# Second attention: the lower half of the mask is added by GpSimd to the rectified scores instead of by TensorE to the scores

## What is computed

```python
def _L1_gnn_ref(hidden, adj, a0, a1, a2, a3):
    def edge_score(a):
        s = jnp.einsum('bid,bjd->bij', hidden * a, hidden)
        return jax.nn.leaky_relu(s, LEAKY_SLOPE)          # slope 0.2
    ...
    alpha = jnp.where(adj == 1, e0, NEG_INF)
    ...
    alpha = jax.nn.softmax(alpha, axis=-1)
    return jnp.matmul(alpha, hidden)
...
x = x + _L1_gnn_ref(_layernorm(x, axis=-1), adj, L1_gnn_a0, ...)
```

## Time and profile before

| what | value |
|---|---|
| median of three runs | 1112.4 us (1112.0 to 1114.0) |
| the profiled execution, first to last instruction (its span; the page gives no other time for it) | 1111.8 us |
| TensorE busy | 1035.5 us, 93% |
| VectorE, ScalarE, GpSimd busy | 678.5, 766.1, 383.3 us |
| `one_kind`, first mask product of batch 0 to 750 us, then 8 us of tail | 466 to 758 us |

### The profile page before, as it was taken

The page is one execution under the profiler, slowest core; times in us unless marked ns, Lnnn a source line. Parts: engine busy times, 40 slices in busy tenths (PEclk is TensorE's granted clock), DMA queues, the critical chain, the costliest instruction groups (busy, mean ns, idle before and its releaser), DMA issues. The chain is left out here.

```text
span 1111.8 us, 19991 instructions
## 1 busy us (share of the span) xinstructions
PE 1035.5 (93%) x6481; PEld 744.2 (67%) x6481; DVE 678.5 (61%) x2122; ACT 766.1 (69%) x1155; POOL 383.3 (34%) x468
## 2 busy tenths in 40 slices
PE   4788789888899999799999999999999999999998
PEld 3455556555477777478888888886466666666667
DVE  4678888778544345288999999772533333333336
ACT  4998798786565554488888888885656556565561
POOL 4113778878573413446565653201000000000000
PEclk9899999899999999899999999999999999999999
DMA  8877987723246665322333232200000000000001
GB/s 290 338 273 272 385 321 294 276 96 125 81 150 228 202 192 169 106 70 83 89 89 89 86 85 74 66 30 1 1 10 11 10 18 12 11 16 14 10 15 33
DMA packets 69145, 131.15 MB, mean 118 GB/s; under 512 B 9918, under 2 KB 30764, under 8 KB 68012
## 3 DMA queue, kind: packets, MB, share of 16 engines
q1 hardware_dynamic: 60268, 111.96, 29.5%
q0 software_dynamic: 8192, 16.79, 5.0%
q10 hardware_dynamic: 576, 1.05, 0.3%
HBM read 77.60 MB, written 52.17 MB: 117 GB/s over the span
## 5 line engine op out<-in xcount | busy, mean ns | idle before, releaser
L2346 PEld LDWEIGHTS eY<-Vo,dGW 128*128 128x128 f32 x1024 | 132.4, 191 | 54.1 <-issue 52.8
L541 POOL DMA_INDIRECT sorted_x<-V,AT_I x128 | 125.5, 980 | 57.8 <-issue 37.0
L2346 PE MATMUL eY<-Vo,dGW 128*128 128x128 f32 x1024 | 134.2, 276 | 0.1
L2329 PE MATMUL eU<-XTN,V 128*128 128x512 f32 x256 | 130.9, 593 | 0.9 <-PEq L2264 0.9
L2516 DVE TENSOR_TENSOR dGW<-H,WBC 128x512 f32<-128x512 f32 x80 | 55.3, 692 | 124.9 <-PE eY L2346 124.7
L2337 PE MATMUL eU<-H,V 128*128 128x512 f32 x256 | 131.1, 594 | 0.0
L730 PE MATMUL O<-Y,HS 128*128 128x512 f32 x256 | 127.6, 618 | 0.0
L1947 POOL DMA_INDIRECT W<-sorted_y,ROW_I x96 | 96.8, 1009 | 73.4 <-PE f_T L2021 53.4
L2425 ACT ACTIVATE H<-eU,bn 128x512 f32<-128x512 f32 x128 | 99.5, 777 | 25.5 <-PE eU L2329 16.2
L2048 PEld LDWEIGHTS f_O<-f_XN,f_PT 128*128 128x128 f32 x896 | 106.8, 192 | 12.7 <-DVE X L2159 10.3
L2048 PE MATMUL f_O<-f_XN,f_PT 128*128 128x128 f32 x896 | 109.8, 276 | 2.6 <-DVE X L2159 2.0
(11 more groups left out here) (306 smaller groups left out, 2069.9 us busy)
## 6 DMA issues: line engine op xcount, KB each, us to landing
XTN<-in_adj SPq DMA_DIRECT2D x64, 512.0 KB, 7.1
masks<-NMW SPq DMA_DIRECT2D x8, 2048.0 KB
f_MK<-masks SPq DMA_DIRECT2D x60, 256.0 KB, 2.7
sorted_y<-zero SPq DMA_DIRECT2D x39, 256.0 KB
NMW<-sorted_x SPq DMA_DIRECT2D x39, 256.0 KB, 2.6
sorted_y<-NMW SPq DMA_DIRECT2D x39, 256.0 KB, 2.5
X<-in_x SPq DMA_DIRECT2D x8, 512.0 KB, 8.0
out_x<-X SPq DMA_DIRECT2D x16, 256.0 KB, 2.3
```

The costliest lines, as they stand in the source:

```text
L541: g_.indirect_dma_start(sorted_x, bass.IndirectOffsetOnAxis(ap=AT_I[b % 2][:, kt:kt + 1], axis=0), XR[b % 2][:, t * P:(t + 1) * P], None). ...
L2329: pe.matmul(U1[j % 2][:, :], V1[:, e * P:(e + 1) * P], XTN[:, b * N + q * HALF:b * N + (q + 1) * HALF], start=True, stop=True).then_inc(u1 ...
L2346: i = pe.matmul(Y[q][:, t * P:(t + 1) * P], GW[:, j % 2, t * P:(t + 1) * P], Vo[:, e * P:(e + 1) * P], start=(e == 0 and t == 0), stop=(e ...
```

## The change

The product `bar` is gone from TensorE. GpSimd adds the lower half of the mask to the lower half of R4, in place (`bar_low`), as VectorE goes on doing with the upper half; the minimum waits for both. The rectification thus sees unmasked scores in both halves. ScalarE's copies of upper blocks now wait for the end of all scores. On GpSimd the lower add of a tile stands ahead of that tile's other work; gathers have lost their own wait for the scores, and the roots stand ahead of the gather of r=4 and r=5 in place of behind that of r=3 and r=4 (in batch 0 the one root moves to r=5).

```diff
@@ gpsimd
+                def bar_low(g):
+                    if g == 0:
+                        pool.wait_ge(late_loaded, 16 * E // 2 * (len(late_loads) + 1))
+                    if g >= RING:
+                        pool.wait_ge(loaded[g % RING], 16 * (g // RING))
+                    pool.wait_ge(r4_ready, g + 1)
+                    nc.gpsimd.tensor_tensor(R4[:, g % 2, 0:HALF], R4[:, g % 2, 0:HALF], mask(g)[:, 0:HALF], ALU.add
+                                            ).then_inc(barred_low, 1)
+
                 for b in range(B):
                     for r in range(NT):
+                        bar_low(b * NT + r)
                         if b + 2 < B:
...
-                            pool.wait_ge(t_ready, b * NT + r + 1)
+                        if r == (5 if b == 0 else 4) and b < LAST:
+                            root(b + 1)
+                        if r == 5 and b > 0:
+                            root_next(b - 1)
+                        if b + 2 < B:
                             gather(b + 2, (r,))
                         if r == 1 and b > 1:
                             feature(b - 2)
-                        if r == 3 and b < LAST:
-                            root(b + 1)
-                        if r == 4 and b > 0:
-                            root_next(b - 1)
@@ tensor, scores(g)
-                    def bar():
...
-                        return pe.matmul(T[g % 2][:, 0:HALF], identb[:, :], mask(g)[:, 0:HALF], start=False, stop=True,
-                                         skip_group_check=(g, 0) in raw_at)
...
-                    half(1)
-                    bar().then_inc(t_ready, 1)
+                    half(1).then_inc(t_ready, 1)
@@ scalar, keep_raw(g, h)
-                    act.wait_ge(raw_ready, raw_at[g, h])
+                    if h == 0:
+                        act.wait_ge(raw_ready, low_at[g])
+                    else:
+                        act.wait_ge(t_ready, g + 1)
@@ vector, shift(g)
                     dve.wait_ge(barred, g + 1)
+                    dve.wait_ge(barred_low, g + 1)
```

More of the change, by code:

```diff
@@ L1879, in one_kind @@
                  "ft_ready", "joined"))
-            barred = either("barred")
+            barred, barred_low = either("barred"), either("tail_barred")
             raw_ready, raw_kept = either("raw_ready"), either("raw_kept")
@@ L1916, in right @@
                 return max(r + 1, 4 * h), 4 * h + 4
-            raw_at = {}
+            raw_at, low_at = {}, {}
             for g_ in range(G):
@@ L1922, in one_kind @@
                         raw_at[g_, h_] = len(raw_at) + 1
+                        if h_ == 0:
+                            low_at[g_] = len(low_at) + 1
             block = ctx.enter_context(nc.Block(no_gpsimd_drain=True))
@@ L2003, in half @@
                         for c in range(4 * h, min(r, 4 * h + 4)):
-                            pe.matmul(T[g % 2][:, c * P:(c + 1) * P], raw(c, r), ident[:, :], start=first,
-                                      stop=False, is_transpose=True)
+                            i = pe.matmul(T[g % 2][:, c * P:(c + 1) * P], raw(c, r), ident[:, :], start=first,
+                                          stop=(c == min(r, 4 * h + 4) - 1 and r >= 4 * h + 4), is_transpose=True)
                             first = False
@@ L2009, in half @@
                             i = pe.matmul(T[g % 2][:, lo * P:(h + 1) * HALF], xta(b)[:, r * P:(r + 1) * P],
-                                          xt(b)[:, lo * P:(h + 1) * HALF], start=first, stop=(h == 1 or (g, 0) in raw_at))
-                            if (g, h) in raw_at:
+                                          xt(b)[:, lo * P:(h + 1) * HALF], start=first, stop=True)
+                            if h == 0 and g in low_at:
                                 i.then_inc(raw_ready, 1)
-                    def bar():
[L2015 to L2020, removed]
-                        return pe.matmul(T[g % 2][:, 0:HALF], identb[:, :], mask(g)[:, 0:HALF], start=False, stop=True,
-                                         skip_group_check=(g, 0) in raw_at)
+                        return i
                     if r > 0:
```

## The result

The changed kernel takes **1173.9 us** (median of four runs, 1172.1 to 1175.2) against 1112.4 before: a ratio of 1.0552, with an interval of 1.0536 to 1.0567. It is slower, and by 61.5 us where 43 were forecast.

The account below looks back on a forecast made before the run. TensorE was taken to set the pace (busy 35.98 of batch 4's 36.32 us), VectorE close behind. Batch changes of +28, +6, +4, +3.6 and +1.2 made +43; 1111.8 + 0.6 + 43 = 1155 us, range 1116 to 1176.

Parts of the forecast that it names:

- Y: Time from the end of rectification to the end of VectorE's minimum; forecast 3.26 us, with TensorE never waiting up to 2.34.
- Rivals 2 and 3: 2: adds exclude each other, VectorE's other work unheld, 1127, chance 0.16; 3: adds side by side, 1105 or 1098, chance 0.09.
- the first case: Mask adds exclude each other and GpSimd's adds hold VectorE's other work: 1155 us, own range 1138 to 1173, chance 0.66.
- The add's price: GpSimd's 512-column lower mask add, taken as 1.27 us by columns between rows of 0.20 and 2.36.
- the ledger: VectorE's own 31.9 us per full batch plus 10.6 to 12.3 lost behind tiles: 42.5 to 44.2, taken as 43.4.
- the ledger's term for r=2: VectorE's loss at tile r=2, 2.7 to 3.3 us: feature sum holds joins for 2.1, then the lower add comes.
- about 38: Batch 0, with neither feature add nor second root, goes from 33.84 us to about 38, +4.
- the loop's 4.6 per tile: Chain from attend through scores, rectification and minimum back to attend: 9.2 us for two tiles, 4.6 each.
- where TensorE has no turns: Batch 7: the reduction taken off the 4.6 against 4.24 per tile, leaving +1.2 us.
- The open point: Whether GpSimd's add also holds VectorE's one-input norms and weighing; if so, r=7 loses 1.1 and the forecast rises some 4 us.
- Late lower adds: GpSimd's lower adds of r=2, r=5 and r=6 queue behind feature, root and gathers; VectorE loses 2.7 to 3.3, 1.3, 3.2 us.
- Rival 5: TensorE's waits lower its granted clock, stretching attend and scores, past 1175 us; chance 0.04.

Follow-up runs that it names:

- run 4: Kernel before, GpSimd's queue in the changed order, plus a 512-column GpSimd add per tile into a spare tile that nobody waits for: 1171.5 us, ratio 1.0522.
- Run 7: Changed kernel without GpSimd's sums of features: 1159.6 us, ratio 1.0403.
- run 8: Changed kernel with the 96 gathers taken off GpSimd; SyncE fetches as many blocks of the same size instead: 1146.9 us, ratio 1.0301.
- run 6: Kernel before, changed GpSimd queue order, spare 512-column GpSimd add that nobody waits for, started when VectorE's mask add has ended: 1136.6 us, ratio 1.0210.
- run 11: Kernel before, feature sum started by the end of the sixth tile's mask add, root job behind it, last batch in the old order: 1110.2 us, ratio 0.9973.
- run 9: Kernel before with GpSimd's feature sum moved from a batch's second tile to its sixth, behind that tile's gathers: 1117.4 us, ratio 1.0037.
- run 1: Changed kernel with GpSimd's lower add replaced by a 512-column fill of a spare tile, same waits, lower mask left out: 1124.1 us, ratio 1.0106.

## Why the prediction was right, and where its size was not

**Direction and mechanism** held. Rectification no longer waits for a mask product, attend waits for "DVE X", joins are held, and the two adds exclude each other: in tiles in which both start together Y is 3.17 (forecast 3.26), though over all tiles its median is 4.18. Rivals 2 and 3 wanted an unheld VectorE or adds side by side; run 4, where nothing waits for GpSimd, loses 58 us all the same, and in 28 of the 29 pairs of mask adds that overlap by more than 0.1 us in the changed kernel one of the two is stretched (together over 2.2 us, against 0.69 + 1.16). One sign failed: GpSimd's add was to have a median of 1.3 to 1.9, and has 1.18; it is stretched in 21 of 64 tiles, and in the other meetings it is VectorE that waits.

**The range** held by little. 1173.9 is 2 us under the top of 1116 to 1176 and 0.9 above the 1138 to 1173 that the first case had for itself; batches of gathers were to last 42 to 44, and three of them lasted 46.3 to 47.5.

**The add's price** was put at 1.27 between 0.20 and 2.36; it is 1.16 to 1.18 alone. The prediction counted a difference in this price 64 times, so the price that was measured, 0.1 lower, would have put its sum some 6 us lower, further from the result. The Trainium skill's estimate (GPSIMD Engine Reference, Performance versus the Vector engine), 1.11, was nearer to the measured price.

**The sum, batch by batch** (from the end of the first rectification to the next such end, batch 7 to its last minimum; us added to before):

| batch | 0 | 1 | 2 | 3 | 4 | 5 | 6 | 7 |
|---|---|---|---|---|---|---|---|---|
| forecast | +4 | +6 | +7 | +7 | +7 | +7 | +3.6 | +1.2 |
| measured | +8.8 | +6.7 | +7.8 | +10.0 | +10.0 | +11.2 | +3.8 | +3.5 |

Batches 1 and 6 came out nearly as worked out. Batch 2 did so in part by luck: the prediction gave it 36.3 before and a feature sum, but it took 35.70, and it has a copy of 1.05 us in the sum's place. Of the 61.8 that were measured, 19 were missing in the forecast; they lie, but for 1.7, in three places.

- *Batches 3 to 5* (10 of them): the step that was sized wrongly is the ledger's term for r=2, "2.7 to 3.3 (feature holds the joins for 2.1, then the lower add comes)". It let VectorE go on between the two; in fact one join waited for both, 3.83 us, Y was 6.6 at r=2 and 6.0 at r=3 (means of batches 3 to 5), and TensorE's clock fell behind the gap. In batch 4 the time from the rectification of r=3 to that of r=4 rose from 4.78 to 9.27 us. Run 7 sizes the term: without the sum that time is 4.95, and the batches take 42.0, which is 4.3 us less in batches 3 and 4 and 5.5 less in batch 5. How much of this is the clock's was not run by itself; the one attend above ran 1.5 longer.
- *Batch 0* (5): the prediction put it at "about 38" and shows no working for it. Here VectorE has six joins behind each of r=1 and r=2 and four behind r=3, some of them held, and Y was 4.4 to 6.4 in tiles 1 to 4; the clock was 0.90. It stays at 42 without gathers on GpSimd (run 8), so adds kept late by gathers are not the cause. It takes 40.1 in run 4, where nobody waits for the add, and 36.2 in run 6, where the same add starts behind VectorE's mask add (33.6 before). So most of it is the meeting; the clock's share, and why it is as dear as that, were not taken apart.
- *Batch 7* (2): the loop's 4.6 per tile and the 4.24 that it replaces both held. From the last minimum of batch 6 to its own, batch 7 took 34.00 before and 37.26 after, 4.25 and 4.66 a tile. Eight times 0.36 is 2.9; what failed is what was then taken off for tiles "where TensorE has no turns", down to 1.2. The runs show 3.3 to 3.5, by where the batch is cut.

**The open point**, whether one-input norms and weighing are held: they are, up to 1.83 and 1.85 us. The Trainium skill's rule (SBUF — State Buffer, Who interferes with whom) says so of one-input instructions in a two-port mode. That these are held agrees with it; whether they run in such a mode no row shows. What it priced at 4 us is in the measured sum, but no run takes it out alone.

**Late lower adds** were named ("lower adds of r=2, r=5 and r=6 now queue behind feature, root and gathers") and put inside the ledger. Run 8 bounds them: 27 us go with the gathers, less held time included, so lateness is a part of these. Rival 5, the clock, had been given 0.04 as a case of its own; it came as a part of the first one (0.90, 0.96, 0.96 and 0.93 in batches 0, 3, 4 and 5).

## What to carry to other kernels

Work handed to an idle GpSimd was not free for VectorE here: with tensors in SBUF on both sides, price it at first as if VectorE had to do it at GpSimd's speed (in run 4, 64 adds of 1.28 us, 82 in all, cost 55), and add each other thing that GpSimd has queued ahead of it. Look in the trace of before for one held instruction, a maximum far over its median beside a GpSimd row: it tells the mechanism, and two GpSimd instructions back to back hold it for both. If GpSimd must add, start it by the end of a VectorE instruction, at a place where VectorE works out of PSUM for as long as the add takes: in run 6 that gave back 35 us, and in run 11 it made the kernel before faster.

## What the runs showed of the hardware that was not expected

- The engine that started first in the record does not always go first. In run 6 VectorE's mask add began at 629.51 and GpSimd's sum at 629.70, and the add ended at 632.64, 0.56 behind the sum's end at 632.08; the join at 604.13 above began 0.19 ahead of the sum and was held all the same. In run 9, where the add began 0.19 behind the sum, it ended 0.55 behind it: a start 0.19 earlier brought it nothing. Whether it was stopped under way or had not begun to read no row shows; GpSimd came straight from a gather each time, and starts on GpSimd are rough. Where GpSimd had been idle and both adds started within 0.05 us, as at 618.49, VectorE kept its time and GpSimd was stretched.
- A fill by GpSimd, which reads nothing, left a two-input add alone (maximum 694 ns), though it lay beside it in full (the two rows below, of run 1). But it held one-input instructions: the weighing at 528.95 took 1.18 us instead of 0.48 beside a fill of 0.54, the norm at 715.85 took 0.77 instead of 0.34 beside one of 0.57.

```profile
500.00 0.69 DVE L2151 TENSOR_TENSOR f_R<-f_R,f_MK 128x512 f32<-128x512 f32 x1 [2.15 <-ACT f_R L2103]
500.01 0.53 POOL L1977 MEMSET f_SCR<- 128x512 f32 x1 [3.85 <-issue]
```

- A full batch with TensorE never waiting takes 35.60 (run 11); the kernel before lost 0.7 of 36.3 in each of four batches to one held join.
